# The seam between attention and the experts: look-up, products with V, first splits and one-hots moved

## The chip, the cores and the metric

One Trainium2 chip, one core. The metric is device time in microseconds of one execution. The engines are TensorE (PE), VectorE (DVE), ScalarE (ACT), GpSimd (POOL) and SyncE (SP), which only issues transfers here.

## The reference

Input 8 x 512 tokens of 256 features, fp32.

```python
xn = layernorm(x)
# differential attention, 16 heads, D = 64, keys and queries of 2 x 64
P = softmax(Q1 K1^T / 8) - lam * softmax(Q2 K2^T / 8)
attn = layernorm(concat(P V) @ Wo + bo) * gamma + beta, times 0.2
# mixture of 8 experts, one per token
routes = argmax(softmax(xn @ switch_w + switch_b))
ffn = prob_max * (gelu(xn @ w1[route] + b1[route]) @ w2[route] + b2[route])
out = x + attn + ffn
```

## The kernel before

Products are made of fp32 parts: a tile is split into a high part (a rounding copy, "high") and a low part (tile minus high, "low"), and three products of parts stand for one.

**Attention's block** (`front_stage`) runs 64 pairs (a batch and two heads), each of 8 steps, 512 steps `g` in all. A step makes the scores of 128 queries on TensorE (`scores`, L945), the negated maxima on VectorE (L836), two exponentials on ScalarE (L604), the reciprocals on VectorE (L796), a scaling of the second softmax `e` on GpSimd (L455), their combination `pm` on VectorE (L803), then four steps later (LAG) transposes on TensorE (L957) and their copy `pT` on ScalarE (L537). Products with V (`times_v`, L972) of a pair come in two halves, in step 5 of the next pair and step 1 of the one after. Their result `p_pv` is copied and split into `oT` (`copy_o` L543, `low_o` L808) and stored by SyncE (`store_o`). In between, the projections of the next pair are made. Each engine has its own queue and executes in the order written; waits on semaphores order the engines.

In steps 452 to 479 VectorE routes the tokens, one small operation a step. In steps 476 to 491 GpSimd makes two one-hots a step (`one_hot`, L422 and L424; 32 in all, each a 128x128 and a 128x46 tile). In steps 504 to 511 TensorE multiplies them, four a step (`find_tokens`, L985, 8 records a step), which gives `token`, the token of each slot of the experts' tiles, copied by VectorE after the last step (L858). Then GpSimd gathers the tokens of tiles 0 and 1 (`gather`, L1059, two transfers a tile). SyncE loads the first weights of the experts in pair 63 (L1052).

Pair 62's halves of products with V are in steps 509 and 510; the transposes of steps 508 to 511 and all of pair 63's products follow the steps.

**The experts' block** (`ffn_and_output_stage`) starts behind a barrier of all engines. It first loads ScalarE's table for Gelu (L1301), splits `w1` of tile 0 on VectorE (L1351 high, L1355 low), and transposes the tokens of tile 0 (L1467), which ScalarE and VectorE split into `xsp` (L1299, L1343). Then 23 tiles of 256 tokens: `hidden` (L1481, 48 products into `p_h`), Gelu and split of `h` (L1315, L1318, L1378), transposes of the next tile, and `outputs` of the tile before (L1494, 48 products into `p_y`). In tile n VectorE also splits `w1` of tile n+1, between the low parts of `h`; ScalarE and GpSimd split `w2` (L1322, L1263). In tile 1 SyncE also issues the loads of `wo`, the rows and four of `x`; the latter wait until all of `oT` is stored. The output stage (L1523) follows.

Of the kernel before, what the change touches and what calls it, by code (L numbers as in the profile page):

```python
# [19 lines left out]
F32 = mybir.dt.float32  # L20
# [10 lines left out]
T = B * S  # L31
# [63 lines left out]
ONE_HOTS_FROM, ONE_HOTS, HOT_FIRST = 476, 2, 4  # L95
# [3 lines left out]
def front_stage(nc, ins, wp_d, xn_d, oT_d, consts, slot_u, prob, tile_expert, token, ahead, s_ost):  # L99
# [3 lines left out]
    with ExitStack() as ctx:  # L103
# [47 lines left out]
        ex = sb("e", [P, EX, 2, S])  # L151
        pm = sb("pm", [P, 4, S])
        (xin,), pTs = then([("xin", [P, NT, E], F32)],
                           [(f"pT{j}{u}", [P, QT, S], F32) for j in range(2) for u in range(2)])
        pT = [pTs[0:2], pTs[2:4]]
        counts = [2 * (b - a) for a, b in TURNS]
        moment_tiles, (oT,) = then([(f"stats{i}", [P, c, 6], F32) for i, c in enumerate(counts)]
                                + [(f"mom{i}", [P, 7, c], F32) for i, c in enumerate(counts)],
                                [("oT", [P, 2, S], F32R)])
        stats, mom = moment_tiles[0:len(TURNS)], moment_tiles[len(TURNS):]  # L160
# [10 lines left out]
        p_token = p_proj[0][:, 0:SC]  # L171
        pC, pR = (p_proj[1][:, a * NT * NE:(a + 1) * NT * NE].rearrange("p (t e) -> p t e", e=NE) for a in range(2))
# [10 lines left out]
        s_ones, s_slots, s_hot, s_table, s_token = (sem(f"r_{x}") for x in ("ones", "slots", "hot", "table", "token"))  # L183
# [26 lines left out]
        PV_FIRST, PV_LAST = 5, 1  # L210

# [7 lines left out]
        def batch_of(pair):  # L219
            return pair // PAIRS  # L220

# [43 lines left out]
        def _(sp):  # L265
# [123 lines left out]
            store_o(NPAIRS - 1)  # L389

        @block.gpsimd
        def _(pool):
# [26 lines left out]

            def one_hot(c):  # L420

                nc.gpsimd.tensor_scalar(low_hot_of(c), marks[:, 0:P], line[:, c:c + 1], None,  # L422
                                        ALU.is_equal)
                nc.gpsimd.tensor_scalar(high_hot[:, c, :], marks[:, P:P + SC], column[:, c:c + 1],  # L424
                                        consts[:, C_TOKEN + c:C_TOKEN + c + 1], ALU.is_equal, ALU.mult
                                        ).then_inc(s_hot, 1)
# [21 lines left out]
            for g in range(STEPS):  # L448
# [1154 lines left out]
```

## Time and profile before

| what | value |
|---|---|
| median of 3 runs | 1900.21 us (1899.0 to 1900.91) |
| profiled execution | 1900.06 us, span 1898.0 us |
| TensorE busy | 97% of the span |
| VectorE, ScalarE, GpSimd busy | 81%, 74%, 38% |
| mean granted clock of TensorE | 0.989 |

The times of rows count from the start of the span. A busy share near 100% says only that an engine always had an instruction in flight; matmuls overlap their successors by some 0.1 to 0.2 us, so the start of the next group is the better measure of what a group takes.

### The profile page before, as it was taken

The numbers are of one execution on the slowest core, as the hardware profiler recorded it, in microseconds if no ns is written. First come the engines' busy times: TensorE is split into PE (matmuls) and PEld (weight loads), VectorE is DVE, ScalarE is ACT, GpSimd is POOL, SyncE is SP. The second block draws the span as 40 slices with busy tenths as digits, with TensorE's granted clock in tenths as the row PEclk, the third lists the DMA queues.
The fourth block names the chain that finished last, engine by engine and source line by source line (L and its number), as shares of the span: only waits on it lengthen the run. The fifth ranks groups of instructions, "written<-read, shape, count | busy, mean of one in ns | idle before, by whom it ended". The sixth has DMA issues, their size and how long they took to land. (4 is left out here: it accounts for less than half of the span.)

```text
span 1898.0 us, 33183 instructions
## 1 busy us (share of the span) xinstructions
PE 1832.6 (97%) x10688; PEld 1423.4 (75%) x10688; DVE 1536.0 (81%) x2562; ACT 1397.8 (74%) x3287; POOL 719.6 (38%) x805
## 2 busy tenths in 40 slices
PE   5899999999999999999999999999999799999997
PEld 4677777777777777777777777777767599999886
DVE  7798888888888888888888888889977476666365
ACT  6798888888888888888888888888777476666100
POOL 4344223232223323323332223332392475554343
PEclk9999999999999999999999999999999799999999
DMA  9998888888888888888888888888876476676998
GB/s 310 252 254 244 237 226 230 226 224 227 233 225 227 229 214 226 225 231 226 228 230 224 226 228 227 229 230 224 211 200 181 138 285 238 235 234 215 310 369 274
DMA packets 226164, 446.11 MB, mean 235 GB/s; under 512 B 27937, under 2 KB 116897, under 8 KB 220001
## 3 DMA queue, kind: packets, MB, share of 16 engines
q1 hardware_dynamic: 220992, 429.86, 81.0%
q0 software_dynamic: 5024, 14.42, 2.5%
q8 instruction: 75, 1.23, 0.3%
q14 instruction: 73, 0.59, 0.1%
HBM read 184.40 MB, written 58.46 MB: 128 GB/s over the span
## 5 line engine op out<-in xcount | busy, mean ns | idle before, releaser
L604 ACT ACTIVATE e<-p_score,nmax 128x512 f32<-128x512 f32 x1024 | 697.2, 689 | 138.6 <-DVE nmax L836 138.2
L455 POOL TENSOR_SCALAR e<-e,rrec,lam 128x512 f32<-128x512 f32 x512 | 393.7, 769 | 948.6 <-DVE rrec L796 948.6
L836 DVE TENSOR_REDUCE nmax<-p_score 128x2 f32<-128x1024 f32 x512 | 623.3, 1217 | 152.7 <-PE p_score L945 150.9
L945 PE MATMUL p_score<-ks,qs 128*128 128x512 f32 x2048 | 578.8, 404 | 8.3 <-DMA ks<-k_parts 5.1
L945 PEld LDWEIGHTS p_score<-ks,qs 128*128 128x128 f32 x2048 | 365.3, 188 | 178.5 <-issue 52.0
L803 DVE SCALAR_TENSOR_TENSOR pm<-e,rrec 128x512 f32<-128x512 f32 x512 | 395.3, 772 | 10.5 <-issue 9.9
L908 PE MATMUL p_proj<-xh,w 128*128 128x512 f32 x1024 | 387.1, 419 | 7.5 <-POOL xl L433 4.6
L537 ACT COPY pT<-p_tr 128x512 f32<-128x512 f32 x512 | 301.0, 588 | 113.8 <-PE p_tr L957 113.8
L957 PE MATMUL p_tr<-consts,pm 128*128 128x128 f32 x2048 | 310.0, 274 | 3.2 <-ACT pT L537 2.3
L957 PEld LDWEIGHTS p_tr<-consts,pm 128*128 128x128 f32 x2048 | 250.2, 141 | 80.2 <-issue 20.0
L972 PE MATMUL p_pv<-pT,v 128*64 128x512 f32 x1024 | 249.2, 608 | 0.7 <-ACT pT L537 0.7
L908 PEld LDWEIGHTS p_proj<-xh,w 128*128 128x128 f32 x1024 | 194.8, 190 | 43.6 <-issue 6.5
L604 ACT ACTIVATION_READ_ACCUMULATOR e<-p_score,nmax 128x1 f32 x1024 | 205.7, 201 | 0.0
L908 PE MATMUL p_proj<-xl,w 128*128 128x512 f32 x512 | 202.2, 395 | 0.0
L1263 POOL TENSOR_TENSOR w2p<-w,w2p 128x2048 fp32r<-128x2048 f32 x23 | 106.8, 4644 | 107.8 <-ACT w2p L1322 107.8
L1481 PE MATMUL p_h<-xsp,w1p 128*128 128x256 f32 x1104 | 134.6, 283 | 8.1 <-DVE xsp L1343 8.1
L1494 PE MATMUL p_y<-w2p,hp 128*128 128x256 f32 x1104 | 139.2, 286 | 2.5 <-POOL w2p L1263 2.5
L1315 ACT ACTIVATE h<-p_h,b 128x256 f32<-128x256 f32 x184 | 76.8, 469 | 86.8 <-PE p_h L1481 83.2
L1481 PEld LDWEIGHTS p_h<-xsp,w1p 128*128 128x128 f32 x1104 | 132.3, 194 | 8.8 <-DVE xsp L1343 8.2
L1494 PEld LDWEIGHTS p_y<-w2p,hp 128*128 128x128 f32 x1104 | 135.1, 193 | 2.7 <-POOL w2p L1263 2.7
L972 PEld LDWEIGHTS p_pv<-pT,v 128*64 128x64 f32 x1024 | 62.5, 137 | 96.9 <-issue 95.8
L1378 DVE TENSOR_TENSOR hp<-h,hp 128x512 fp32r<-128x512 f32 x92 | 64.7, 704 | 61.1 <-ACT hp L1318 57.7
(158 smaller groups left out, 1876.5 us busy)
## 6 DMA issues: line engine op xcount, KB each, us to landing
ks<-k_parts SPq DMA_DIRECT2D x512, 256.0 KB, 4.6
qs<-q_parts SPq DMA_DIRECT2D x512, 128.0 KB, 4.4
w<-weight_parts_scratch SPq DMA_DIRECT2D x56, 1024.0 KB, 10.6
w<-in_w SPq DMA_DIRECT2D x46, 1024.0 KB, 6.7
oT_scratch<-oT SPq DMA_DIRECT2D x64, 512.0 KB, 6.2
op<-oT_scratch SPq DMA_DIRECT2D x32, 1024.0 KB, 10.2
wv<-weight_parts_scratch SPq DMA_DIRECT2D x56, 256.0 KB, 5.6
weight_parts_scratch<-w SPq DMA_DIRECT2D x8, 1024.0 KB, 6.3
```

Of the source, the lines that this page charges most:

```text
L455: nc.gpsimd.tensor_scalar(e2, e2, rrec[:, g % 4, 1:2], lam[:, 0:1], ALU.mult, ALU.mult).then_inc(s_e2, 1)
L537: nc.scalar.copy(pT[pair % 2][st // QT][:, :, qt * P:(qt + 1) * P], p_tr[:, :, :]).then_inc(s_pT, 1)
L604: nc.scalar.activation(ex[:, g % EX, m, :], p_score[g % 2][:, m, :], ACT.Exp, bias=nmax[:, g % 2, m:m + 1], accum_out=rsum[:, g % 4, m:m + ...
L803: vec.scalar_tensor_tensor(out=pm[:, g % 4, :], in0=ex[:, g % EX, 0, :], scalar=rrec[:, g % 4, 0:1], in1=ex[:, g % EX, 1, :], op0=ALU.mult ...
L836: vec.tensor_reduce(nmax[:, g % 2, :], p_score[g % 2][:, :, :], AXX, ALU.max, negate=True).then_inc(s_max, 1)
L908: last_op = nc.tensor.matmul(bank[:, :], weights(j, a, what[0], u, k), x_part(batch, b, k, 0, S), start=(k == 0 and c == 0), stop=(k == KT ...
L945: last_op = nc.tensor.matmul(p_score[g % 2][:, m, :], qs[j][u][:, m, qt * P:(qt + 1) * P], ks[j][u][:, m, part, :], start=(part == 0), sto ...
L957: last_op = nc.tensor.transpose(p_tr[:, k, :], pm[:, g % 4, k * P:(k + 1) * P], ident)
L972: last_op = nc.tensor.matmul(p_pv[u * D:(u + 1) * D, :], v[it % 2][:, k, c:c + D], pT[j][u][:, k, :], start=(k == 0), stop=(k == QT - 1))
L1263: nc.gpsimd.tensor_tensor(w2p[j][:, 1, :, :], w2[j][:, :, :], w2p[j][:, 0, :, :].bitcast(F32), ALU.subtract).then_inc(s_w2lo, 1)
L1481: last_op = nc.tensor.matmul(p_h[g % 2][:, f % 2, :], w1p[j][:, a, k, f * P:(f + 1) * P], xsp[j][:, b, k, :], start=(k == 0 and c == 0), s ...
L1494: last_op = nc.tensor.matmul(p_y[j][:, s, :], hp[j][:, a, f, s * P:(s + 1) * P], w2p[j][:, b, f, :], start=(f == 0 and c == 0), stop=(f == ...
```

## The change

- One-hots: GpSimd makes 24, one a step from 476 to 499; VectorE the other 8, one in every third step from 476 to 497.
- `find_tokens` takes place in steps 504, 506, 507 and 508, 8 one-hots (16 records) each; `token` is copied in step 509, and the two gathers of tile 0 are issued by GpSimd behind the scalings of `e` of steps 508 and 509, the two of tile 1 behind the last step.
- Pair 62's products with V leave steps 509 and 510 and stand between the transposes of steps 508 to 510. The copy of pair 62's `oT` moves along.
- In attention's block, behind the last step: ScalarE makes the high parts of `w1` of tiles 0 and 1, the high part of tile 0's tokens and loads the Gelu table; VectorE makes the low parts; TensorE transposes tile 0's tokens between the transposes of steps 510 and 511. The experts' tile 0 splits no `w1`.
- Pair 63's product with V stays in its bank; it is copied, split and stored in tile 1 of the experts' block.
- Tiles of SBUF: `oT` and `warm` are placed before everything else, `e` where the moments were with `oT`; `xsp` and `p_x` are placed so that both blocks can use them.

```diff
-ONE_HOTS_FROM, ONE_HOTS, HOT_FIRST = 476, 2, 4
+ONE_HOTS_FROM, HOT_FIRST = 476, 4
+POOL_HOTS = 24
...
+        FIND_AT = (0, 2, 3, 4)
...
+        def one_hot(engine, c, s_done):
+            engine.tensor_scalar(low_hot_of(c), marks[:, 0:P], line[:, c:c + 1], None, ALU.is_equal)
+            engine.tensor_scalar(high_hot[:, c, :], marks[:, P:P + SC], column[:, c:c + 1],
+                                 consts[:, C_TOKEN + c:C_TOKEN + c + 1], ALU.is_equal, ALU.mult).then_inc(s_done, 1)
...
@@ sync, end of the block @@
             store_o(NPAIRS - 2)
-            store_o(NPAIRS - 1)
@@ gpsimd, step g @@
-                if 0 <= g - ONE_HOTS_FROM < NT // ONE_HOTS:
+                if 0 <= g - ONE_HOTS_FROM < POOL_HOTS:
                     if g == ONE_HOTS_FROM:
                         pool.wait_ge(s_slots, 1)
                         pool.wait_ge(s_marks, 16)
-                    for c in range(ONE_HOTS * (g - ONE_HOTS_FROM), ONE_HOTS * (g - ONE_HOTS_FROM + 1)):
-                        one_hot(c)
-            pool.wait_ge(s_token, 1)
-            ahead.gather(pool, 0)
-            ahead.gather(pool, 1)
+                    one_hot(nc.gpsimd, g - ONE_HOTS_FROM, s_hot)
+                if g == STEPS - 4:
+                    pool.wait_ge(s_token, 1)
+                    ahead.gather(pool, 0, 0)
+                if g == STEPS - 3:
+                    ahead.gather(pool, 0, 1)
+            for s in range(FS):
+                ahead.gather(pool, 1, s)
@@ scalar, after the steps @@
-                if g == STEPS - 1:
-                    copy_o(NPAIRS - 2)
...
-            for g in range(STEPS - LAG, STEPS):
-                copy_pT(g)
-            copy_o(NPAIRS - 1)
+            def w1_high(n):
+                act.wait_ge(ahead.landed["w1"][n], 16)
+                for k in range(KT):
+                    nc.scalar.copy(ahead.tiles["w1p"][n][:, 0, k, :], ahead.tiles["w1"][n][:, k, :]
+                                   ).then_inc(ahead.s_w1hi, 1)
+                    yield
+
+            first, second = w1_high(0), w1_high(1)
+            copy_pT(STEPS - 4)
+            act.wait_ge(s_table, 1)
+            act.wait_ge(s_route, 1)
+            next(first)
+            copy_pT(STEPS - 3)
+            next(first)
+            copy_o(NPAIRS - 2)
+            copy_pT(STEPS - 2)
+            act.wait_ge(ahead.s_tr, 1)
+            nc.scalar.copy(ahead.xsp[0][:, 0, :, :], ahead.p_x[0][:, :, :]).then_inc(ahead.s_xhi, 1)
+            copy_pT(STEPS - 1)
+            next(second)
+            next(second)
+            nc.scalar.activation(ahead.warm[:, :], consts[:, 0:4], ACT.Gelu_apprx_tanh)
@@ vector, step g and after @@
-                if g == STEPS - 1:
-                    low_o(NPAIRS - 2)
+                if g >= ONE_HOTS_FROM and (g - ONE_HOTS_FROM) % 3 == 0:
+                    c = POOL_HOTS + (g - ONE_HOTS_FROM) // 3
+                    if c == POOL_HOTS:
+                        dve.wait_ge(s_slots, 1)
+                        dve.wait_ge(s_marks, 16)
+                    if c < NT:
+                        one_hot(vec, c, s_hot_dve)
+                if g == STEPS - 3:
+                    dve.wait_ge(s_table, 1)
+                    vec.tensor_copy(token[:, :], p_token).then_inc(s_token, 1)
...
-            dve.wait_ge(s_table, 1)
-            vec.tensor_copy(token[:, :], p_token).then_inc(s_token, 1)
             combine(STEPS - 1)
-            low_o(NPAIRS - 1)
+            w1_low(0)
+            low_o(NPAIRS - 2)
+            dve.wait_ge(ahead.s_xhi, 1)
+            vec.tensor_tensor(ahead.xsp[0][:, 1, :, :], ahead.p_x[0][:, :, :], ahead.xsp[0][:, 0, :, :].bitcast(F32),
+                              ALU.subtract).then_inc(ahead.s_xlo, 1)
+            w1_low(1)
@@ tensor @@
+                    pe.wait_ge(s_hot, POOL_HOTS)
+                    pe.wait_ge(s_hot_dve, NT - POOL_HOTS)
+                for c in range(NT // 4 * quarter, NT // 4 * (quarter + 1)):
...
+            def first_transposes():
+                pe.wait_ge(s_token, 1)
+                pe.wait_ge(ahead.landed["xs"][0], 16 * FS)
...
-                if st == PV_FIRST and pair >= 1:
+                if st == PV_FIRST and 1 <= pair < NPAIRS - 1:
                     times_v(pair - 1, (0, 1))
...
-                if g == STEPS - 2:
-                    times_v(NPAIRS - 2, (2, 3))
-                if pair == NPAIRS - 1:
-                    find_tokens(st)
+                if pair == NPAIRS - 1 and st in FIND_AT:
+                    find_tokens(FIND_AT.index(st))
...
-            for g in range(STEPS - LAG, STEPS):
-                transposes(g)
+            transposes(STEPS - 4)
+            times_v(NPAIRS - 2, (0, 1))
+            transposes(STEPS - 3)
+            times_v(NPAIRS - 2, (2, 3))
+            transposes(STEPS - 2)
+            first_transposes()
+            transposes(STEPS - 1)
             times_v(NPAIRS - 1, range(QT))
@@ experts' block: sync, scalar, vector, in tile 1 @@
                 if t.exact and n == 1:
+                    sp.wait_ge(ahead.s_last_lo, 1)
+                    sp.dma_start(oT_d[PAIRS - 1, :, :, T - S:T], ahead.oT[:, :, :].bitcast(F32)).then_inc(s_oT, 16)
                     first_of_output()
...
+                if t.exact and n == 1:
+                    act.wait_ge(ahead.s_last_pv, 1)
+                    act.wait_ge(s_oT, 16 * (B * PAIRS - 1))
+                    nc.scalar.copy(ahead.oT[:, 0, :], ahead.p_last[:, :]).then_inc(ahead.s_last_hi, 1)
...
-                    if t.has(1):
+                    if t.has(1) and t.after(1):
                         if g < KT:
                             w1_high(n + 1, 1 - j, t.half_next, g, not t.after(1))
...
+                if t.exact and n == 1:
+                    dve.wait_ge(ahead.s_last_hi, 1)
+                    v.tensor_tensor(ahead.oT[:, 1, :], ahead.p_last[:, :], ahead.oT[:, 0, :].bitcast(F32), ALU.subtract
+                                    ).then_inc(ahead.s_last_lo, 1)
```

## Rows read from the trace of the kernel before

**Rows 1.** The page, busy time and share of the span of each engine

```profile
...
PE 1832.6 (97%) x10688; PEld 1423.4 (75%) x10688; DVE 1536.0 (81%) x2562; ACT 1397.8 (74%) x3287; POOL 719.6 (38%) x805
...
```

**Rows 2.** Timeline of TensorE, seam: start us, us, instruction, count [idle before <- releaser]

```profile
...
1447.19 1.09 PE L985 MATMUL p_proj<-high_hot,low_hot 128*128 128x46 f32 x8
...
1460.73 1.94 PE L972 MATMUL p_pv<-pT,v 128*64 128x512 f32 x8
...
1467.84 1.18 PE L945 MATMUL p_score<-ks,qs 128*128 128x512 f32 x4
...
1477.46 5.08 PE L972 MATMUL p_pv<-pT,v 128*64 128x512 f32 x16 [0.67 <-ACT pT L537]
1485.13 0.63 PE L1467 MATMUL p_x<-consts,xs 128*128 128x128 f32 x4 [2.60 <-PEq L103]
1489.42 7.86 PE L1481 MATMUL p_h<-xsp,w1p 128*128 128x256 f32 x48 [3.67 <-DVE xsp L1343]
...
1501.74 8.58 PE L1481 MATMUL p_h<-xsp,w1p 128*128 128x256 f32 x48 [4.02 <-DVE xsp L1343]
...
1510.51 6.00 PE L1494 MATMUL p_y<-w2p,hp 128*128 128x256 f32 x48
1516.34 5.67 PE L1481 MATMUL p_h<-xsp,w1p 128*128 128x256 f32 x48
...
```

**Rows 3.** Timeline of GpSimd, steps 478 and 479

```profile
...
1377.96 0.77 POOL L455 TENSOR_SCALAR e<-e,rrec,lam 128x512 f32<-128x512 f32 x1
...
1381.09 0.77 POOL L455 TENSOR_SCALAR e<-e,rrec,lam 128x512 f32<-128x512 f32 x1
...
```

**Rows 4.** Timeline of TensorE, scores of step 3 of pairs 55, 56, 59 and 62

```profile
...
1270.44 1.09 PE L945 MATMUL p_score<-ks,qs 128*128 128x512 f32 x4
...
1292.58 1.09 PE L945 MATMUL p_score<-ks,qs 128*128 128x512 f32 x4
...
1361.58 1.09 PE L945 MATMUL p_score<-ks,qs 128*128 128x512 f32 x4
...
1432.38 1.09 PE L945 MATMUL p_score<-ks,qs 128*128 128x512 f32 x4
...
```

**Rows 5.** One-hots on GpSimd: x count: ns least/median/most, first and last start

```profile
...
L422 POOL TENSOR_SCALAR low_hot<-marks,line x32: 592/602/1077, 1372.0 to 1420.7; 128x128 f32<-128x128 f32 x32
...
L424 POOL TENSOR_SCALAR high_hot<-marks,column,consts x32: 522/530/724, 1372.6 to 1421.2; 128x46 f32<-128x46 f32 x32
...
```

**Rows 6.** The page, costliest groups: busy, mean ns | idle before, releaser

```profile
...
L604 ACT ACTIVATE e<-p_score,nmax 128x512 f32<-128x512 f32 x1024 | 697.2, 689 | 138.6 <-DVE nmax L836 138.2
...
L836 DVE TENSOR_REDUCE nmax<-p_score 128x2 f32<-128x1024 f32 x512 | 623.3, 1217 | 152.7 <-PE p_score L945 150.9
...
```

**Rows 7.** Timeline of ScalarE, expert tiles 0 and 2

```profile
...
1499.25 1.90 ACT L1322 CAST w2p<-w 128x2048 fp32r<-128x2048 f32 x1
...
1523.62 0.58 ACT L1299 CAST xsp<-p_x 128x512 fp32r<-128x512 f32 x1
...
```

**Rows 8.** TensorE by stretches of 1 us: busy, granted clock, DMA share, GB/s

```profile
...
1485.00:1486.00 1.00, 0.63 (x4) 1.00 0.90 344
...
1501.00:1502.00 1.00, 0.26 (x1) 0.50 0.00 0
...
```

**Rows 9.** Timeline of SyncE's queue, tile 2

```profile
...
1522.57 1.49 SPq L1052 DMA_DIRECT2D w<-in_w  x2
...
```

**Rows 10.** Timeline of VectorE, tile 3

```profile
...
1534.05 0.68 DVE L1351 CAST w1p<-w 128x1024 fp32r<-128x1024 f32 x1
...
```

**Rows 11.** Timeline of GpSimd, gathers

```profile
...
1474.17 1.33 POOL L1059 DMA_INDIRECT xs<-xn_scratch,slot_token  x1 [0.94 <-DVE slot_token L858]
...
1532.13 8.09 POOL L1059 DMA_INDIRECT xs<-xn_scratch,slot_token  x1 [0.30 <-issue]
...
1556.63 1.00 POOL L1059 DMA_INDIRECT xs<-xn_scratch,slot_token  x1 [0.30 <-issue]
...
```

**Rows 12.** Gathered tokens, all 46: time from issue to landing

```profile
...
DMA to landing us min/median/max: 2.8/6.5/10.9
...
```

More of the change, by code:

```diff
@@ L182, in front_stage @@
         s_wqhi, s_wqlo, s_wst = sem("w_qhi"), sem("w_qlo"), [sem(f"w_st{j}") for j in range(2)]
-        s_ones, s_slots, s_hot, s_table, s_token = (sem(f"r_{x}") for x in ("ones", "slots", "hot", "table", "token"))
+        s_ones, s_slots, s_hot, s_table, s_token, s_hot_dve = (sem(f"r_{x}") for x in ("ones", "slots", "hot", "table", "token", "hot_dve"))
         s_marks = sem("r_marks")
@@ L856, in _, with w1_low @@
             combine(STEPS - 2)
-            dve.wait_ge(s_table, 1)
-            vec.tensor_copy(token[:, :], p_token).then_inc(s_token, 1)
             combine(STEPS - 1)
-            low_o(NPAIRS - 1)
+            def w1_low(n):
+                for k in range(KT):
+                    dve.wait_ge(ahead.s_w1hi, KT * n + k + 1)
+                    w1p = ahead.tiles["w1p"][n]
+                    vec.tensor_tensor(w1p[:, 1, k, :], ahead.tiles["w1"][n][:, k, :], w1p[:, 0, k, :].bitcast(F32),
+                                      ALU.subtract).then_inc(ahead.s_w1lo, 1)
+            w1_low(0)
[4 more added lines that the diff above has]
+            w1_low(1)
         @block.tensor
@@ L1044, in __init__ @@
             self.tiles["b1"], self.tiles["b2"] = two("b1", [P, FT]), two("b2", [P, E])
+            two("w2p_place", [P, 2, FT, E])
+            self.xsp = two("xsp", [P, 2, KT, FFN_TILE], F32R)
+        with ExitStack() as early:
+            for bank in range(6):
+                early.enter_context(nc.psum_tensor(f"bank{bank}", [P, S], F32))
+            self.p_x = [early.enter_context(nc.psum_tensor(f"p_x{j}", [P, KT, FFN_TILE], F32)) for j in range(2)]
     def expert(self, sp, n):
@@ L1054, in load, with gather @@
             sp.dma_start(dst[:, :], src.rearrange("a p f -> (a p) f")).then_inc(self.landed[name][j], 16)
[L1056 to L1062 removed]
+    def gather(self, pool, n, s):
+        c = n * FS + s
+        pool.indirect_dma_start(
+            out=self.tiles["xs"][n % 2][s][:, :], out_offset=None, in_=self.xn_d,
+            in_offset=bass.IndirectOffsetOnAxis(ap=self.token[:, c:c + 1], axis=0)
+        ).then_inc(self.landed["xs"][n % 2], 16)
 def ffn_and_output_stage(nc, ins, ys_d, oT_d, consts, tile_expert, slot_u, prob, ahead, s_oT, out):
@@ L1096, in ffn_and_output_stage @@
         w2p = [sb(f"w2p_{j}", [P, 2, FT, E], F32R) for j in range(2)]
-        xsp = [sb(f"xsp{j}", [P, 2, KT, FFN_TILE], F32R) for j in range(2)]
+        xsp, p_x = ahead.xsp, ahead.p_x
+        sb("xsp_home", [P, 2, 2, KT, FFN_TILE])
         (h,), acc = then([("h", [P, HG, 2, FFN_TILE], F32)], [(f"acc{r}", [P, 2, E], F32) for r in range(R)])
@@ L1108, in ffn_and_output_stage @@
         mom = [sb(f"omom{a}", [P, 6, 4]) for a in range(2)]
-        warm = sb("warm", [P, 4])
-        p_x = [ps(f"p_x{j}", [P, KT, FFN_TILE]) for j in range(2)]
+        warm = ahead.warm
         p_h = [ps(f"p_h{a}", [P, 2, FFN_TILE]) for a in range(2)]
@@ L1255, in gather @@
                 pool.wait_ge(s_tr, n - 1)
-                ahead.gather(pool, n)
+                for s in range(FS):
+                    ahead.gather(pool, n, s)
             for n in range(FFN_TILES):
@@ L1497, in outputs @@
                 last_op.then_inc(s_y, 1)
-            transposes(0, 0, 0, True)
             def body(t):
```

70 lines of the change are left out of this document (30 added, 40 removed).

## The prediction

> **What bounds the kernel now.** I read the page first: TensorE is busy 97% of the span [rows 1], so only places where it stands, or where another engine sets its pace, are worth anything. Its share falls in one place, around the seam between the attention block and the experts' block. The timeline of TensorE over the seam [rows 2] shows the order there: the last scores start at 1467.84, the last products with V at 1477.46 and end at 1482.54, the first transposes of gathered tokens start at 1485.13, expert tile 0 at 1489.42, tile 1 at 1501.74, tile 0's second product at 1510.51. From there on TensorE is the bound again, tile after tile, so what is saved before 1510.51 is kept to the end.
>
> A second place is hidden in the busy shares. In steps 476 to 491 GpSimd executes its scaling of `e` and two one-hots per step. Its scalings start at 1377.96 and 1381.09, so 3.13 us apart [rows 3], with nothing idle between them: GpSimd is the pace-maker. The price shows on TensorE. The scores of step 3 of two successive pairs, before any routing work, are at 1270.44 and 1292.58: 22.14 us a pair. Those of steps 475 and 499, three pairs apart, are at 1361.58 and 1432.38, which is 70.80 us where 66.4 would do [rows 4]. So about 4.4 us are lost there.
>
> **One-hots on two engines.** After the change GpSimd does one per step for 24 steps: 0.77 us of scaling plus 0.60 for the 128x128 and 0.53 for the 128x46 one [rows 3, 5], 1.90 us of a 2.77 us step. It no longer sets the pace. VectorE gets eight, one every third step. The trace has no such operation on VectorE. From below the bound is nothing (it has idle time in most steps); from above GpSimd's own 0.60 + 0.53 each, 9 us in all, of which perhaps a third would meet a step in which VectorE has no slack (two reductions back to back). VectorE's short operations in this trace are far cheaper than GpSimd's, so I take 0.3 us each, 2.4 in all, of which 0.3 us reaches TensorE. Term: 4.4 - 0.3 = **4.1 us**; bounds 1.4 and 4.4. The waits for the slots and marks at step 476 are long satisfied; they cost nothing, and `find_tokens` now waits for all 32 at step 504, four steps after the last is made.
>
> **Scores of pair 63.** Before, TensorE has no idle time from 1447.19 to 1467.84: 20.65 us. A group of 8 look-up records takes 0.8 to 0.9 us net [rows 2], one follows each step. The change puts 16 records into steps 504, 506, 507 and 508, which is one group more ahead of the last scores (+0.5 net of the waits they had), and takes the two halves of pair 62's product with V out of steps 509 and 510, each 1.94 us less overlap, 1.86 net (-3.7), and 0.2 of other overlap. TensorE would be ready for the last scores 3.4 us earlier, at 1464.4. But those scores need the exponentials of step 509: its scores at 1461.5, 1.2 us for them, 1.2 for the reduction, 1.4 for the two exponentials [rows 6] gives 1465.4. Term: 1467.84 - 1465.4 = **2.4 us**.
>
> **The tail.** Before, TensorE waits between the transposes of steps 508 to 511 for the `pT` copies and for `pm`; 9.6 us pass from the last scores to the last products with V. After: transposes of 508 at about 1468.2 (the `pT` copy of 507 is behind an exponential), half of pair 62's product (to 1470.5), transposes 509, the other half (to 1472.9), transposes 510, the first transposes of tokens (1473.3), transposes 511 at 1474.15, their copy to 1475.4. So 1465.4 to 1475.45 is 10.05 us: **-0.45 us**, though 3.7 us of products and the token transposes are now inside. ScalarE's insertions are two copies of 128x1024 of `w1`. The trace has no such copy there; 128x512 takes 0.57 to 0.58 and 128x2048 1.90 [rows 6, 7], so 1.0 each, between 0.9 and 1.2. They fit beside the products (1470.1 to 1472.7), and so does `copy_o` of pair 62. The last products, 16 records, took 5.08 us, where pair 62's, two groups of 8, took 1.86 net each [rows 2]: 3.75, **+1.3 us**. The difference is the granted clock. Behind them nothing of pair 63 is copied any more: the 2.55 us from the end of the products to the barrier's end (2.60 idle) [rows 2] shrink to some 0.65, **+1.9 us**; by 1478.9 ScalarE has split tile 1's `w1` and loaded its table, and VectorE has subtracted.
>
> **First expert tiles.** After the barrier TensorE had to wait 3.67 us more on top of 0.63 of transposes for `w1p` and `xsp`: 4.3 us from 1485.13 to 1489.42. Both are there already: **+4.3 us**. Sum so far for tile 0's start: 2.4 - 0.45 + 1.3 + 1.9 + 4.3 = 9.5, at 1479.9. From tile 0 to tile 1 it took 12.3 us, partly at half clock and with tile 1's weights split between the subtractions. In an undisturbed tile the `xsp` copy starts 7.28 us after the tile (1516.34 to 1523.62 [rows 2, 7]), 0.6 for it and 0.65 for the low part, so 8.75 with the queue: **+3.6 us**. Tile 1 to tile 0's second product took 8.77 us at mostly half clock; full 5.85. The granted clock was 0.50 (1.2 of 2.4 GHz) at the start of tile 1, after 4.02 us idle; behind the 2.60 idle before 1485.13 it was still 1.00 [rows 2, 8]. The wait that is left before tile 1 is 2.8 us, between these: I take half of 2.9, **+1.45 us**, bounds 0 and 2.9. And because the waits of the tail are still there, only shorter, I take **-0.7** for a low clock in them, bounds 0 and -2. GpSimd's `w2p` of tile 0 is ready 14.45 us after tile 0's start, TensorE wants it at 14.6: no loss, with no slack.
>
> **Queues that are moved past.** SyncE's last store of `oT` moves to tile 1, in front of `wo`, the rows and four loads of `x`, and these loads wait for its landing. The loads of tile 3 and 4's weights behind them start at 1522.57 [rows 9], which is 12.1 us after tile 0's second product; they would go 2 to 4 us later. VectorE wants that `w1` at 1534.05 [rows 10]. The earlier issue leaves 11.5 us for a landing of some 8. I take 0.0, bound -2.5. GpSimd's queue: the first two gathers stand in front of the scalings of steps 509, 510 and 511. At 1.33 and about 1.0 us plus 0.3 of issue [rows 11] the last `pm` comes at 1471.8, 2.4 us before its transposes can run: nothing. The second gather is issued at 1468.2 and wanted at 1473.3; landings take 2.8, 6.5 and 10.9 us (least, median, most) [rows 12], and the loads of `w1` and `w2` have drained by then, so I take 4: in time.
>
> **Sum.** 9.5 + 3.6 + 1.45 + 4.1 - 0.7 = 17.95. The profiled execution took 1900.06 us (span 1898.0), 0.15 under the median of 1900.21, so the forecast is 1900.2 - 17.9 = 1882.3 us.
>
> **Rivals.**
> (a) Gathers hold up GpSimd. One of 46 took 8.09 us on the engine, at 1532.13, while VectorE had no pause [rows 11]. If a gather moves only while VectorE stands, the first one ends when VectorE runs out of work for want of `e` (1468.1), and the chain slips: last products 0.9 us later, 1883.2. If one takes its 8.09 whole, 7.0 more less 2.4 of slack: 1886.9. If the second lands after 10.9 us, at 1479.1 instead of 1473.3: 1888.1. Against it: the gather at 1556.63 took 1.00 beside an equally busy VectorE. The Trainium skill, "SBUF — State Buffer", section "SBUF: two separate sides", says that a transfer issued by GpSimd waits for its descriptors while VectorE runs a two-port operation such as an fp32 copy between SBUF tiles. By that rule the moved gathers, which stand beside reductions from PSUM, would hardly be held, and the `w1` copies that could hold them go to ScalarE; the trace agrees in one row and not in the other.
> (b) The one-hots give nothing: the pace is handed to VectorE at 3.1 us a step. Then 1886.4. Against it: a step of VectorE is 1.2 of reduction, 0.7 of combination and 0.1 of reciprocal, and 22.14 us for eight steps is what TensorE takes when nobody holds it [rows 4].
> (c) The low clock holds through the tail, tile 0 and tile 1: the 1.45 of tile 1, 1.3 of the last products and 1.6 of tile 0's first group are lost, 1886.7.
> (d) The change doesn't do what it says: the seam hands its wait on, because `w2p` on GpSimd or SyncE's late loads are late instead; 2.5 to 5 us given back, 1885 to 1887.
> (e) Slower. The layout of SBUF moves for all 512 steps (`e`, `pm`, `pT` have new places). A step takes 2.77 us. If each grew by 0.035 us, by conflicts between engines at the new addresses, the 17.9 us would be gone; beyond that the kernel is slower, and at 0.05 us a step it would take 1882.3 + 25.6 = 1907.9. Nothing in the trace shows that a place matters; no instruction of a step is changed.
>
> **How the numbers follow.** Forecast 0.58 (its own range 1879 to 1885.5), (a) 0.12, (b) 0.07, (c) 0.10, (d) 0.09, (e) 0.04. The best case adds the clock's 2.15 and the one-hots' 0.3: 1879.9; two bounds at once on the bad side reach 1889. Range 1878 to 1889.5. A difference of 0.2%, 3.8 us, is about what a measurement of this kernel can tell from none. Faster 0.94, same 0.03, slower 0.03: all cases but (e) are beyond the bound.
>
> **What the changed profile would show.** The scalings of `e` on GpSimd follow VectorE's reciprocals again in steps 476 to 499, and steps 475 to 499 take 66.4 to 67 us. No products with V between the last scores. Token gathers on GpSimd before the last two scalings, about 1 us each. Less than 1.2 us between the last product with V and the first `p_h`. Tile 0 to tile 1 about 8.8 us; tile 1 either 5.9 or up to 8.8 to `p_y`, by the clock. The prediction fails if a gather stands for several us in front of a scaling, if tile 1 or a later tile waits for a weight, or if the steps before 476 have another length than now.

## The result, and the profile after

| what | before | after |
|---|---|---|
| median | 1900.91 us (1899.0 to 1903.19, 7 runs) | 1888.0 us (1884.65 to 1893.09, 7 runs) |
| profiled execution | 1900.06 us, span 1898.0 | 1892.03 us, span 1889.9 |
| mean granted clock | 0.989 | 0.993 |

The ratio is 0.9935, 95% interval 0.9921 to 0.9949: 12.9 us faster between the medians, where 17.9 were forecast. The page still has TensorE at 97%:

```profile
...
PE 1825.8 (97%) x10688; PEld 1419.8 (75%) x10688; DVE 1540.0 (81%) x2574; ACT 1402.2 (74%) x3291; POOL 710.9 (38%) x789
...
```

The timeline of TensorE after, which answers to [rows 2] and [rows 4] (start us, us, instruction, count, idle before and what ended it; the last line is tile 3, cut off by the end of the view):

```profile
...
1362.92 1.10 PE L984 MATMUL p_score<-ks,qs 128*128 128x512 f32 x4
...
1429.20 1.09 PE L984 MATMUL p_score<-ks,qs 128*128 128x512 f32 x4
...
1462.68 1.20 PE L984 MATMUL p_score<-ks,qs 128*128 128x512 f32 x4 [0.96 <-ACT e L605]
...
1472.82 3.65 PE L1011 MATMUL p_pv<-pT,v 128*64 128x512 f32 x16 [0.67 <-ACT pT L540]
1476.96 5.68 PE L1547 MATMUL p_h<-xsp,w1p 128*128 128x256 f32 x48 [0.49 <-PEq L104]
...
1485.70 5.92 PE L1547 MATMUL p_h<-xsp,w1p 128*128 128x256 f32 x48 [2.62 <-DVE xsp L1411]
...
1491.82 6.00 PE L1560 MATMUL p_y<-w2p,hp 128*128 128x256 f32 x48
1502.21 7.24 PE L1547 MATMUL p_h<-xsp,w1p 128*128 128x256 f32 x48 [4.40 <-DVE xsp L1411]
...
1515.48 4.70 PE L1547 MATMUL p_h<-xsp,w1p 128*128 128x256 f32 x40
...
```

From such starts the span divides into stages. Tile n's first product is its `p_h`, its second is `p_y`. "Again" is a second profiled run of the same kernel after; it is one of the experiments.

| stage (from start to start, us) | before | after | again |
|---|---|---|---|
| to step 475 | 1361.58 | 1362.92 | 1359.59 |
| steps 475 to 499 | 70.80 | 66.28 | 66.23 |
| step 499 to tile 0's `p_h` (the seam) | 57.04 | 47.76 | 47.76 |
| tile 0 to tile 1 | 12.32 | 8.74 | 8.74 |
| tile 1 to tile 0's `p_y` | 8.77 | 6.12 | 7.64 |
| to tile 2 | 5.83 | 10.39 | 5.83 |
| tile 2 to tile 3 | 11.69 | 13.27 | 11.68 |
| tile 3 to the last tile's `p_y` | 227.38 | 227.00 | 227.17 |
| from there to the end | 142.59 | 147.42 | 146.66 |

Three things are to be seen. The stretch that was costed, down to tile 0's second product, gained 4.52 + 9.28 + 3.58 + 2.65 = 20.0 us, more than the forecast. In the profiled execution 6.1 us are lost again in tile 2, behind a wait of 4.40 us that the kernel before doesn't have. And the end of the kernel, which no edit touches, is 4.8 us longer, in the second run 4.1. With 1.3 us more ahead of step 475 (step 475 starts between 1359.2 and 1364.9 over the profiled executions of all these kernels; why is open) and 0.4 less over the other tiles the sum is 8.1, the difference of the two spans.

**The wait in tile 2.** The engines' timelines lead to it. GpSimd after:

```profile
...
1463.01 1.10 POOL L1121 DMA_INDIRECT xs<-xn_scratch,slot_token  x1 [0.16 <-issue]
...
1486.69 4.62 POOL L1330 TENSOR_TENSOR w2p<-w,w2p 128x2048 fp32r<-128x2048 f32 x1 [7.05 <-ACT w2p L1386]
...
1495.52 4.95 POOL L1330 TENSOR_TENSOR w2p<-w,w2p 128x2048 fp32r<-128x2048 f32 x1 [1.56 <-ACT w2p L1386]
...
```

VectorE after, the same stretch:

```profile
...
1489.00 2.87 DVE L1440 TENSOR_TENSOR hp<-h,hp 128x512 fp32r<-128x512 f32 x1 [3.35 <-ACT hp L1382]
...
1495.99 5.56 DVE L1423 TENSOR_TENSOR w1p<-w,w1p 128x1024 fp32r<-128x1024 f32 x1
1501.48 0.68 DVE L1411 TENSOR_TENSOR xsp<-p_x,xsp 128x512 fp32r<-128x512 f32 x1
...
```

All executions of these two VectorE instructions (count, then ns least/median/most, first and last start):

```profile
...
L1440 DVE TENSOR_TENSOR hp<-h,hp x92: 673/692/2869, 1480.2 to 1744.4; 128x512 fp32r<-128x512 f32 x92
...
L1423 DVE TENSOR_TENSOR w1p<-w,w1p x42: 1206/1220/5561, 1494.3 to 1733.6; 128x1024 fp32r<-128x1024 f32 x42
...
```

In tile 1 the first low part of `h`, which usually takes 0.69 us, takes 2.87; the last one of `w1`, which usually takes 1.22, takes 5.56. Both began while GpSimd's 128x2048 subtraction was under way, and ended 0.6 and 1.1 us after its end (1491.31, 1500.47), about their own length. So both look as if VectorE had stood until GpSimd's instruction was over; the experiments test this. The `xsp` behind the second is what TensorE waited for. The Trainium skill, "SBUF — State Buffer", section "SBUF: two separate sides", describes such a lock: the port pair that GpSimd and VectorE share goes to one instruction for its whole length when VectorE reads two SBUF operands against a GpSimd instruction that reads SBUF. The two rows agree. In the kernel before, GpSimd's first subtraction (1501.23 to 1505.80) fell into a gap in VectorE's work:

```profile
...
1501.23 4.57 POOL L1263 TENSOR_TENSOR w2p<-w,w2p 128x2048 fp32r<-128x2048 f32 x1 [11.64 <-ACT w2p L1322]
...
```

**The one-hots**, which answer to [rows 5]:

```profile
...
L227 POOL TENSOR_SCALAR low_hot<-marks,line x24: 600/608/615, 1373.7 to 1436.5; 128x128 f32<-128x128 f32 x24
L227 DVE TENSOR_SCALAR low_hot<-marks,line x8: 278/281/284, 1369.3 to 1427.1; 128x128 f32<-128x128 f32 x8
...
```

The other half of each, from the view of `high_hot`:

```profile
...
L228 DVE TENSOR_SCALAR high_hot<-marks,column,consts x8: 301/303/307, 1369.5 to 1427.3; 128x46 f32<-128x46 f32 x8
...
```

### The profile page after: what moved, and what is told of

It is laid out like the page before. It is cut to its first block and busy times, and to the rows that moved or that the text cites. A ratio compares the mean times of both kernels' runs of the same rounds, so it can differ in the third digit from the quotient of the medians.

```text
span 1889.9 us, 33187 instructions
## 1 busy us (share of the span) xinstructions
PE 1825.8 (97%) x10688; PEld 1419.8 (75%) x10688; DVE 1540.0 (81%) x2574; ACT 1402.2 (74%) x3291; POOL 710.9 (38%) x789
```

## Experiments on the wait in tile 2

**The kernel after once more** (`after_again`, no edit).

> The changed kernel once more, unchanged. The seven runs of it lie between 1884.7 and 1893.1. Theory: stretches up to the last second product repeat within 0.5 us, the wait of 4.4 us before tile 2 is there again, and what differs is the output stage, whose groups took 8.05 us in the profiled execution and 7.76 in that of the kernel before. Rival: the spread is in the seam (the 4.4 us is there in some executions only).

Measured: 1883.44 us, span 1881.3. The wait wasn't there. TensorE:

```profile
...
1482.32 7.45 PE L1547 MATMUL p_h<-xsp,w1p 128*128 128x256 f32 x48 [2.62 <-DVE xsp L1411]
...
1489.96 5.99 PE L1560 MATMUL p_y<-w2p,hp 128*128 128x256 f32 x48
1495.79 5.67 PE L1547 MATMUL p_h<-xsp,w1p 128*128 128x256 f32 x48
...
```

VectorE, then GpSimd:

```profile
...
1485.88 2.55 DVE L1440 TENSOR_TENSOR hp<-h,hp 128x512 fp32r<-128x512 f32 x1 [3.62 <-ACT hp L1382]
...
1492.57 1.21 DVE L1423 TENSOR_TENSOR w1p<-w,w1p 128x1024 fp32r<-128x1024 f32 x1
1493.70 0.67 DVE L1411 TENSOR_TENSOR xsp<-p_x,xsp 128x512 fp32r<-128x512 f32 x1
...
```

```profile
...
1493.66 4.63 POOL L1330 TENSOR_TENSOR w2p<-w,w2p 128x2048 fp32r<-128x2048 f32 x1 [3.13 <-ACT w2p L1386]
...
```

Here the granted clock fell in tile 1 (0.78 over its stretch, 1.00 in the first run), whose `p_h` took 7.45 us where it had taken 5.92. That loses 1.5 us and saves 6.1. The first lock is there in this run too (2.55 us); the second is not, because ScalarE's work in tile 1, and GpSimd's behind it, comes later against VectorE's queue: GpSimd's second subtraction (1493.66) starts only as VectorE's last `w1` split ends (1493.78). The `xsp` beside it, with one operand in PSUM, takes its usual 0.67 us under the same GpSimd instruction, so it is not the engine as a whole that is slowed. My theory that every execution has the wait fell; what remained is that it depends on whether the clock holds through tile 1. Why the clock holds in one execution and not in the other, after the same work and the same wait of 2.62 us, is not shown. The margin in the first run was 0.5 us (1495.99 against 1495.52).

**An eighth of GpSimd's first subtraction** (`w2low0_one_row`). It leaves out 7 of the 8 rows of the low part of tile 0's `w2`; tile 0's second product reads the high part in their place, at the same length.

```diff
-                nc.gpsimd.tensor_tensor(w2p[j][:, 1, :, :], w2[j][:, :, :], w2p[j][:, 0, :, :].bitcast(F32),
+                rows = 1 if n == 0 else FT
+                nc.gpsimd.tensor_tensor(w2p[j][:, 1, 0:rows, :], w2[j][:, 0:rows, :],
...
```

> Leaves out 7 of 8 rows of the low part of w2 of tile 0 (GpSimd's subtraction is an eighth as long), and tile 0's second product reads the high part in its place, so only tile 0's precision is lost. Theory of the two engines that hold one another up: GpSimd's instruction takes 0.6 us, ends before VectorE's first low part of tile 1, both long VectorE instructions of tile 1 are gone, tile 2 starts 5.8 to 6.0 us after tile 0's second product. Rival (transfers): they stay.

Measured: 1880.61 us, span 1878.6. TensorE:

```profile
...
1481.88 5.92 PE L1548 MATMUL p_h<-xsp,w1p 128*128 128x256 f32 x48 [2.62 <-DVE xsp L1412]
...
1487.99 5.99 PE L1561 MATMUL p_y<-w2p,hp 128*128 128x256 f32 x48
1493.82 5.66 PE L1548 MATMUL p_h<-xsp,w1p 128*128 128x256 f32 x48
...
```

The clock held through tile 1 (5.92) as in the first run of after, and there is no wait: tile 1 to tile 2 is 11.94 us where it was 16.51. VectorE's low part of `h` has its 0.69 us back, its queue runs some 2 us earlier, and its last `w1` split ends 0.2 us ahead of GpSimd's second subtraction:

```profile
...
1485.17 0.69 DVE L1441 TENSOR_TENSOR hp<-h,hp 128x512 fp32r<-128x512 f32 x1 [3.35 <-ACT hp L1383]
...
1490.30 1.22 DVE L1424 TENSOR_TENSOR w1p<-w,w1p 128x1024 fp32r<-128x1024 f32 x1
...
```

This shows the chain: with the clock held, the first lock (2.2 us) pushes VectorE into the second (4.3 us), and without the first there is no second, though GpSimd's second subtraction is as long as before.

**The same subtraction on VectorE** (`w2low0_on_dve`), computation unchanged; GpSimd only signals it.

```diff
@@ gpsimd @@
+                if n == 0:
+                    pool.wait_ge(s_w2lo_dve, 1)
+                    nc.gpsimd.memset(tick[:, :], 0.0).then_inc(s_w2lo, 1)
+                    continue
@@ vector, tile 0 @@
+                if t.exact and n == 0:
+                    dve.wait_ge(s_w2hi, 1)
+                    v.tensor_tensor(w2p[0][:, 1, :, :], w2[0][:, :, :], w2p[0][:, 0, :, :].bitcast(F32),
+                                    ALU.subtract).then_inc(s_w2lo_dve, 1)
```

> The low part of w2 of tile 0 is made by VectorE, in the pause it has after the low part of tile 1's tokens, not by GpSimd. Theory (in the changed kernel GpSimd's 4.6 us subtraction of tile 0 now runs under VectorE's low parts of tile 1, one of which takes 2.87 us instead of 0.69, and that pushes VectorE into the subtraction of tile 1, where a split of w1 takes 5.56 us instead of 1.22): no VectorE instruction of tile 1 over 1.3 us, tile 2 starts without a wait at 5.8 to 6.0 us after tile 0's second product instead of 10.4, and takes 5.6 instead of 7.2 us; about 6.1 us less than the changed kernel, some 1882. Rival (VectorE is slowed by transfers landing in SBUF, or waits for tile 2's w1): the 5.56 us stays, the time stays at 1888.

Measured: 1884.67 us (1882.25 to 1890.21, 5 runs), ratio 0.9918 (0.9902 to 0.9934). Tile 2 does not wait. But in its profiled execution the clock was low in tile 1 (7.65 us to `p_y`), where after has no wait either, so this run alone doesn't tell the theories apart. The later run with both remedies (`dve_and_32_bytes`) does. The forecast of some 1882 was 2.7 us too low.

**The subtractions of tiles 0 and 1 in eight pieces** (`w2low_pieces`), to let VectorE in between them.

```diff
+                pieces = 8 if n < 2 else 1
+                for q in range(pieces):
+                    a, b = q * FT // pieces, (q + 1) * FT // pieces
+                    last_op = nc.gpsimd.tensor_tensor(w2p[j][:, 1, a:b, :], w2[j][:, a:b, :],
...
```

> GpSimd's subtraction of w2 for tiles 0 and 1 in 8 pieces of 0.6 us instead of one of 4.6. If an instruction of VectorE waits for the end of the one GpSimd instruction that is running, no VectorE instruction of tile 1 takes more than its own time plus 0.6; GpSimd's eight then take longer in sum (they wait for VectorE in turn) and tile 0's second product starts up to 2 us late; tile 2 starts 2 to 4 us earlier than in the changed kernel, counted from tile 0. If VectorE is slowed by transfers, its 5.56 us stays.

Measured: 1886.0 us, span 1884.0. Eight pieces take 6.96 and 6.11 us of GpSimd where one takes 4.62, and tile 0's `p_y` now comes 0.35 us late (8.00 us behind tile 1, 7.65 with the clock alone). No VectorE instruction waits more than 0.6 us. Tile 2 doesn't wait, but the clock was low here too, where after has no wait either; so this run shows that the pieces free VectorE and what they cost GpSimd, not that they cure the wait.

## Experiments on the end of the kernel

In the output stage the DMA engines are full. TensorE's groups come in pairs (one tile `op` of 256 tokens); the first of each pair waits for it. TensorE after:

```profile
...
1831.67 0.50 PE L1583 MATMUL p_o<-bop,ones_r 1*128 1x256 f32 x2 [1.12 <-DMA op<-oT_scratch]
...
1835.12 0.50 PE L1583 MATMUL p_o<-bop,ones_r 1*128 1x256 f32 x2
...
1839.73 0.50 PE L1583 MATMUL p_o<-bop,ones_r 1*128 1x256 f32 x2 [1.09 <-DMA op<-oT_scratch]
...
```

A pair takes 8.06 us, of which the waited step is 4.61; in the kernel before it is 4.31, and TensorE alone needs 3.45. The length of the whole end is a rougher measure: at one and the same place of the tiles it was 145.7 to 148.1 us in eight profiled executions (after's place), and 142.6 and 144.5 in two (before's). What moved is the place of the tiles: `oT` (4096 bytes a partition) and `warm` (16) now stand in front of everything. By the order and sizes of the tiles, `op` starts at 448 bytes past a multiple of 512 before and at 480 after, and `x`, `acc` and `ff` at a multiple of 512 before and 32 past it after.

**The kernel before with after's places** (`before_32_bytes_on`). One unused tile of 32 bytes is put ahead of the others.

```diff
         token = sb("slot_token", [P, SC], U32)
+        gap = sb("gap", [P, 8])
```

> The kernel before, with an unused tile of 32 bytes in front, so that every tile of SBUF behind it has the address remainder that it has in the changed kernel (tiles of the output stage: 32 bytes past a multiple of 64, where they were at a multiple). Theory of the addresses: the output stage's groups of two alternate 3.45 and 4.6 us instead of 3.45 and 4.31, the stretch from the last second product to the end grows from 142.6 to 145.5 to 147.5 us, nothing before changes. Rival (the output stage differs from run to run, or by what lies before it in the changed kernel): 142.6 stays within 1 us.

Measured: 1903.36 us (beside it, the kernel before 1901.24). In the last third of the stage the waited step is 4.55 to 4.62 us; the end is 146.92.

**The kernel after, 32 bytes on** (`after_32_bytes_on`): `op` at a multiple of 512, `x`, `acc` and `ff` 64 past one.

```diff
-        oT, warm = sb("oT", [P, 2, S], F32R), sb("warm", [P, 4])
+        oT, warm = sb("oT", [P, 2, S], F32R), sb("warm", [P, 12])
```

> The changed kernel with its first new tile 32 bytes longer, so that the output stage's tiles start at a multiple of 64 bytes again. Theory of the addresses: the groups alternate 3.45 and 4.31 us again, last second product to end 142.6 to 143.5 us instead of 146 to 147.5, some 4 us less in all: 1884 and 1880 by the state of tile 2's wait. Rival: no difference.

Measured: 1881.57 us (1875.6 to 1884.47, 5 runs), ratio 0.9894 (0.9876 to 0.9911). The waited step is 3.87 to 4.13 us, the end 139.22. Expected was the kernel before's 4.31 us; it came out below that, so a multiple of 64 bytes is not all there is to it.

**The kernel before at those places** (`before_64_bytes_on`: the unused tile is 64 bytes).

> The kernel before with an unused buffer of 64 bytes a partition ahead of the output stage's, so that the buffers that hold the rows of the attention's output begin at a multiple of 512 bytes (as in the kernel after with 32 bytes on), where the kernel before has them at 448 past one. If the start address of the buffers sets what a group's transfers take: gaps between the output stage's groups of 3.9 to 4.05 us in place of 4.31, the stretch from the last tile's second product to the end 139 to 140.5 us in place of 142.6, and a time of 0.997 to 0.999 of the kernel before; then the placement is worth the same without the change, and the change alone, both kernels placed well, is worth what lies between this kernel and the one after with 32 bytes on (some 15 to 17 us). If it was something else in the kernel after (its look-up's place in time, its longer buffer): gaps of 4.3 and no change.

Measured: 1896.37 us (1894.62 to 1897.82, 6 runs), ratio 0.9971 (0.9959 to 0.9983); waited step 3.94 to 4.08, end 138.30. So 32 or 64 unused bytes move the end by 8.6 us between worst and best without an edit to the computation. At the same places the two kernels' ends are within 1 us of each other (146.92 and 147.42; 138.30 and 139.22), so the change has hardly a part in it but the place.

Windows of 40 us, all in the part where the DMA engines are full, show it as a rate (busy us of PE, PEld, DVE, ACT, POOL, then granted clock, DMA share, GB/s). Before:

```profile
...
1820.00:1860.00 40.00, 37.19 (x282) 34.22 (x283) 21.91 (x74) 0.62 (x3) 17.59 (x16) 1.00 1.08 370
...
```

After:

```profile
...
1810.00:1850.00 40.00, 34.52 (x260) 31.48 (x259) 19.09 (x71) 0.62 (x3) 15.30 (x15) 1.00 1.08 357
...
```

Before with 32 bytes:

```profile
...
1824.00:1864.00 40.00, 35.66 (x257) 32.50 (x257) 20.14 (x74) 0.62 (x3) 15.25 (x15) 0.96 1.08 357
...
```

After with 32 bytes:

```profile
...
1796.00:1836.00 40.00, 38.21 (x289) 34.98 (x289) 23.28 (x77) 0.41 (x2) 16.27 (x15) 1.00 1.08 386
...
```

Before with 64 bytes:

```profile
...
1814.00:1854.00 40.00, 39.02 (x295) 35.92 (x295) 25.20 (x84) 0.41 (x2) 17.03 (x15) 1.00 1.08 387
...
```

The DMA share is the same, 1.08, in all five; the rate goes by the place alone: 357 GB/s for both kernels at one, 386 and 387 for both at another. In stretches of 10 us from 1800 to 1850 the levels stay apart: 353 to 361, 367 to 373 and 384 to 390. The Trainium skill, "DMA: Bandwidth & Descriptors", section "How a descriptor splits into AXI transactions", says that the first transaction of a descriptor which doesn't start at a multiple of 256 bytes starts at the multiple below, and that the bytes ahead of the start are fetched for nothing. It doesn't say that this holds for a start in SBUF that is written to. The order agrees for `op` (best at 0). For `x`, `acc` and `ff` it doesn't: they are 64 bytes past a multiple where the rate is best, and at one where it is 370. Which of `op`, `x`, `acc` and `ff` makes how much of it was not separated, and neither was why 448 and 480 bytes past a multiple of 512 differ by 13 GB/s; that `x` and its like moved from a multiple to 32 past it may be that part. A placement of the kernel after 224 bytes further on, which was to tell a multiple of 64 from one of 256, didn't fit into SBUF, so that question is open.

## Experiments on the terms of the sum

**The one-hots alone in the kernel before** (`before_new_onehots`: `POOL_HOTS`, the loop of GpSimd and the insertion in VectorE of the diff, the rest as before).

> The kernel before with the one-hots of the change alone: 24 on GpSimd, one a step, 8 on VectorE. Expected: steps 475 to 499 take 66.3 us instead of 70.8, everything else as before, so 4.5 us less: 0.9976 of the kernel before. If the pace of those steps were set by TensorE or VectorE, no gain.

Measured: 1897.25 us (9 runs), ratio 0.9977 (0.9967 to 0.9988). Steps 475 to 499 take 66.22 us, the seam behind them 57.10 as before.

**Pair 62's products back between the last scores** (`pv62_in_scores`).

```diff
@@ tensor @@
-                if st == PV_FIRST and 1 <= pair < NPAIRS - 1:
+                if st == PV_FIRST and pair >= 1:
...
+                if g == STEPS - 2:
+                    times_v(NPAIRS - 2, (2, 3))
...
             transposes(STEPS - 4)
-            times_v(NPAIRS - 2, (0, 1))
             transposes(STEPS - 3)
-            times_v(NPAIRS - 2, (2, 3))
```

> The kernel after, but the two halves of pair 62's product with V stand before the scores of steps 510 and 511 again, as in the kernel before. By the prediction's terms: TensorE comes to the last scores 2.5 to 2.9 us later (3.7 us of products less the 0.96 us that the kernel after waits there), and the stretch from there to the last products shrinks by only 0.5 to 1.1 us from 10.14 us, because the waits for the pT copies come back where the products had stood: seam from step 499 to tile 0's first product 49.2 to 50.2 us in place of 47.76. If the order of these products doesn't matter (the same work in either place): 47.8 to 48.3. Tile 0 to 1 8.74 in both cases.

Measured: 1895.76 us, span 1893.8, seam 51.82 us, 4.06 longer. TensorE:

```profile
...
1464.51 1.19 PE L984 MATMUL p_score<-ks,qs 128*128 128x512 f32 x4
...
1474.18 5.31 PE L1011 MATMUL p_pv<-pT,v 128*64 128x512 f32 x16 [0.68 <-ACT pT L540]
1479.97 5.68 PE L1547 MATMUL p_h<-xsp,w1p 128*128 128x256 f32 x48 [0.49 <-PEq L104]
...
1488.71 5.92 PE L1547 MATMUL p_h<-xsp,w1p 128*128 128x256 f32 x48 [2.62 <-DVE xsp L1411]
...
1505.22 7.28 PE L1547 MATMUL p_h<-xsp,w1p 128*128 128x256 f32 x48 [4.40 <-DVE xsp L1411]
...
```

Its clock, in windows over the tail and the last products (columns: busy us of PE, granted clock, DMA share, GB/s):

```profile
...
1466.00:1474.00 8.00, 4.22 (x22) 0.79 0.15 44
1474.00:1479.00 5.00, 4.82 (x16) 0.65 0.30 113
...
```

The last scores come 2.88 us later behind step 499, as expected, and the tail shrinks by 0.47, where 0.5 to 1.1 were. Not expected were the other 1.66: the last products take 5.31 us at a clock of 0.65, where they take 3.65 in after. TensorE was busy for 5.7 of the tail's 9.7 us, and the clock fell; in after it is busy for 8.2 of 10.1 and the clock stays at 1.00. The other runs bear this out: with the products in the tail the last ones take 3.65 us in all nine profiled executions, without them 5.08 to 6.43 in the four of the kernel before and its variants. So the products in the tail are worth their order and, beyond it, the clock of what follows. The clock was whole again in tiles 0 and 1 (5.68, 5.92), and the 4.40 us wait returned with it, as the theory of the lock says.

**Pair 63's output stored from attention's block again** (`last_o_in_seam`).

```diff
@@ sync @@
+            store_o(NPAIRS - 1)
@@ scalar, behind w1_high of tile 1 @@
+            act.wait_ge(ahead.s_last_pv, 1)
+            act.wait_ge(s_ost, 16 * (NPAIRS - 1))
+            nc.scalar.copy(oT[:, 0, :], p_pv[:, :]).then_inc(s_ohi, 1)
@@ vector, behind w1_low(1) @@
+            low_o(NPAIRS - 1)
```

(and the three places in tile 1 of the experts' block are taken out)

> The kernel after, but pair 63's output copied, split and stored in attention's block, before its closing barrier, as in the kernel before. By the prediction's term for the barrier: seam from step 499 to the first product of tile 0 longer by 1.9 us (49.6 to 49.9 in place of 47.76), tile 0 to 1 8.7 to 8.8, the wait for tile 1's activation gone or shorter since ScalarE and VectorE have no copy there. If the barrier doesn't wait for it (the copy ends behind the look-up's last work anyway): 47.8, unchanged.

Measured: 1888.1 us, span 1886.2; seam 50.03 us, 2.27 longer. TensorE waits 2.74 us at the barrier in place of 0.49, and the clock is then low in tiles 0 and 1 (0.77), so that tile 0 to tile 1 takes 10.31, where 8.7 to 8.8 were expected:

```profile
...
1475.81 7.41 PE L1542 MATMUL p_h<-xsp,w1p 128*128 128x256 f32 x48 [2.74 <-PEq L104]
...
1486.12 7.46 PE L1542 MATMUL p_h<-xsp,w1p 128*128 128x256 f32 x48 [2.47 <-DVE xsp L1410]
...
```

**Tile 1's `w1` split in the experts' block again** (`w1_of_tile1_in_ffn`).

```diff
@@ scalar, attention's block @@
-            next(second)
-            next(second)
@@ vector, attention's block @@
-            w1_low(1)
@@ vector, experts' block @@
-                    if t.has(1) and t.after(1):
+                    if t.has(1):
```

> The kernel after, but tile 1's w1 split where the kernel before has it, behind tile 0's work in the experts' block. By the prediction's term for it: seam unchanged at 47.7 to 47.8 (the splits had lain under the last products), tile 0 to 1 9.9 to 12.3 in place of 8.74 (VectorE's two splits of 1.2 us and ScalarE's halves return behind tile 0's), the rest as after. If ScalarE's two halves had held up the look-up: seam shorter by up to 1 us. If the splits weren't on the path: 8.7 to 8.8.

Measured: 1889.61 us, span 1887.8; seam 47.78, tile 0 to tile 1 10.24 us, 1.50 longer:

```profile
...
1476.80 5.69 PE L1544 MATMUL p_h<-xsp,w1p 128*128 128x256 f32 x48 [0.49 <-PEq L104]
...
1487.04 7.45 PE L1544 MATMUL p_h<-xsp,w1p 128*128 128x256 f32 x48 [4.12 <-DVE xsp L1408]
...
```

**Both remedies in the kernel after** (`dve_and_32_bytes`: tile 0's low part of `w2` on VectorE, and `warm` with 12 columns).

> The kernel after with both remedies: the low part of tile 0's w2 on VectorE, and 32 bytes in front of the output stage's buffers. If the two causes add: steps 475 to 499 in 66.2, seam 47.8, tile 0 to 1 8.7, tile 1 to tile 0's second product 6.1 to 8 (by the clock), then 5.83 and 11.7 with no wait in tile 2, output stage's gaps 3.94 to 4.04, end 139 to 140; a median of 1877 to 1881 and a ratio to the kernel before of 0.988 to 0.990. If the two aren't of one another free (VectorE's 5 us of subtraction late for tile 0's second product): that of 32 bytes alone, 0.9894, or worse.

Measured: 1876.38 us (1874.44 to 1877.12, 4 runs), ratio 0.9862 (0.9847 to 0.9877). It is the fastest version here, 25 us under the kernel before, 20 us under the kernel before at the same places (measured beside it). TensorE:

```profile
...
1483.36 5.92 PE L1556 MATMUL p_h<-xsp,w1p 128*128 128x256 f32 x48 [2.47 <-DVE xsp L1416]
...
1489.47 5.99 PE L1569 MATMUL p_y<-w2p,hp 128*128 128x256 f32 x48
1495.31 5.66 PE L1556 MATMUL p_h<-xsp,w1p 128*128 128x256 f32 x48
...
```

This time the clock held through tile 1, the case in which after waits 4.40 us, and tile 2 follows without a wait. VectorE's own subtraction takes half of GpSimd's 4.62 us:

```profile
...
1484.30 2.29 DVE L1456 TENSOR_TENSOR w2p<-w,w2p 128x2048 fp32r<-128x2048 f32 x1 [0.99 <-ACT w2p L1391]
...
```

## Why the prediction was right, and what it missed

The sign, the range and the mechanism held; the median is 5.7 us above the forecast of 1882.3. That the range (1878 to 1889.5) holds it is in part luck: two losses that aren't in the sum, 10.9 us together in the profiled execution, are there in full only in some executions, and three of the seven runs lie above the range. Step by step, from the profiled execution:

| term | predicted | measured |
|---|---|---|
| one-hots | 4.1 | 4.5 (alone: 4.58 by the stage, 4.4 by its ratio) |
| scores of pair 63 | 2.4 | 1.98 |
| tail | -0.45 | -0.52 |
| last products | +1.3 | +1.4 |
| barrier and first tile | 1.9 + 4.3 | 6.4 |
| tile 0 to tile 1 | 3.6 | 3.58 |
| tile 1 to `p_y` | 1.45 | 2.65, and 1.13 in the second run |
| low clock in the tail | -0.7 | 0 |
| sum | 17.95 | 20.0, and 18.6 |
| tile 2's wait and clock | 0 | -6.1, and 0 |
| output stage | 0 | -4.8, and -4.1 |

**One-hots.** VectorE's cost was mis-sized: a one-hot takes 0.28 + 0.30 = 0.58 us where 0.3 was taken. None of it reached TensorE, though, where 0.3 us were set down for it, and the steps themselves take 22.09 us a pair, not 22.14, so the term came out 0.4 larger. Rival (b), the pace handed to VectorE, is refuted.

**The seam.** It gained 9.28 us; the five terms add up to 9.45, which the prediction rounded to 9.5. Its length is the same within 0.02 us in all executions of kernels that have the change whole. The last scores wait for `e`, not for TensorE's queue, as predicted (0.96 us in the timeline; 1.0 in the prediction). The gathers of tile 0 took 1.10 and 1.03 us on GpSimd, and TensorE's token transposes didn't wait for them: rival (a) is refuted. The barrier term is shown by the run that undoes it (2.27, 1.9 predicted), the `w1` splits by theirs (1.50 of the 3.58 from tile 0 to tile 1; the rest goes with the clock in tile 0, whose `p_h` takes 5.68 us where it took 7.86), and the place of pair 62's products by theirs (4.06, of which 1.66 is clock). What the prediction missed there is that these aren't independent: in these runs a wait brought back in the tail or at the barrier also took the clock from the next group.

**Tile 1's clock.** Half of 2.9 was a mean of two cases which both occur, 2.65 and 1.13.

**The step that failed first** is "GpSimd's `w2p` of tile 0 is ready 14.45 us after tile 0's start, TensorE wants it at 14.6: no loss, with no slack". It was ready in time (1491.31, wanted at 1491.82). The loss came from whom it held up: with tile 1 no longer late, GpSimd's instruction starts 1.0 us behind tile 1's first product, where it started 0.5 ahead of it, and so falls on VectorE's, not into a gap. The prediction had taken the overlap of the two engines as free. That is rival (d), a wait handed on, but on another engine than it named and at 6.1 us, not 2.5 to 5. It occurs when tile 1 runs at the full clock, which two profiled executions in this form showed (after and `pv62_in_scores`) and four at the low clock did not. (In this form: GpSimd's subtractions as in after.) That the seven runs of after lie at 1884.65 to 1888.0 and at 1892.03 to 1893.09 fits two cases some 5 us apart, but so does the stretch ahead of step 475, which alone differs by 5.7 us; those without a profile don't show which it was.

**The step that failed second** is "Nothing in the trace shows that a place matters". Rival (e) had the cause, the moved layout, and looked for it in conflicts per step. The steps are no longer: eight of them take 22.09, 22.08, 22.07 and 22.13 us at 240, 640, 1040 and 1260 us of the span, 22.08, 22.08, 22.06 and 22.15 in the kernel before. What depends on the place is the rate of transfers, and it sets the time only where the DMA engines are the bound, the output stage: -4.8 us. SyncE's moved queue, the other wait that was feared, cost nothing: tile 3 to the last tile takes 227.0 us against 227.4.

Without the two, 20.0 us; with the place alone 15.2, with both 9.1; the measured 12.9 lies between. Rival (c), the low clock throughout, didn't occur; tile 1 alone had it in some executions.

## What to carry to other kernels

When a stage is pulled forward, list which instructions of the other engines now run at the same time, not only whether each is ready in time: GpSimd and VectorE can each be ready and still lock each other out. Try several start addresses for tiles that are loaded in a stage bound by transfers (here `op` at a multiple of 512 bytes was best), and after any edit of the allocation compare the rate of that stage. A wait of TensorE that is removed is worth itself and, often, the clock of the next group, so fill unavoidable waits with products that have to be made anyway.

## What the runs showed of the hardware that was not expected

- A VectorE subtraction of two SBUF tiles that starts under a GpSimd subtraction ends only after it: 2.87 us for 0.69, 5.56 us for 1.22. One with an operand in PSUM isn't held: 0.67 us.
- VectorE subtracts 128x2048 fp32 in 2.29 us, GpSimd in 4.62; in eight pieces GpSimd needs 6.1 to 7.0.
- With full DMA engines the rate went from 357 to 387 GB/s by the tiles' start addresses alone.
- A low clock in tile 1 lost 1.5 us there and saved 6.1 us in tile 2, because it shifted two engines against each other: 4.6 us less in all.
